# One megakernel of two attention, expert and feed-forward layers on one Trainium2 core: grouped keys, more PSUM banks for the experts, the convolution as matmuls

## The reference, cut to what matters

```python
x = x + attn0(cond(x, mask, cond_256, Wq, Wk, Wv, Wo, ...))     # cond: 16 heads of 8; attn0: 16 heads of 64, rotary, causal
x = x + moe0(rotate(x, ...))                                    # 8 experts, top 2, 128 -> 512 -> 128, relu
x = x + attn1(moe1(x, ...))                                     # moe1: 8 experts, top 2, 128 -> 256 -> 256 -> 128; attn1: 8 heads, decay
x = x + ffn(cond(x, ...))

def cond(...):                                  # in both places
    scores = einsum('bhsd,bhtd->bhst', q, k) * scale            # 16 heads of 8 features, 32 positions
    attn = softmax(where(mask, -inf, scores))
    out = einsum('bhst,bhtd->bhsd', attn, v) @ Wo.T
    return out / rms(out) * rms_scale * (1 + sc) + shift

def ffn(x, w1, conv_w, conv_b, w2):
    h = bit_linear(x, w1)            # row of x rounded to 127 steps of its largest value, weights to -1, 0, 1; 128 -> 512
    h = silu(depthwise_conv1d(h, conv_w, conv_b))               # 3 taps along the 32 positions
    return bit_linear(h, w2)                                    # 512 -> 128
```

## Time and profile before

| what | us |
|---|---|
| median of 3 runs (lowest, highest) | 674.3 (670.13, 675.94) |
| the profiled execution's own time | 680.54 |
| span of the profiled execution, first to last instruction | 678.7 |
| busy: PE, PEld, DVE, ACT, POOL | 468.1, 363.8, 350.4, 269.8, 212.3 |
| mean granted TensorE clock | 0.825 of 2.4 GHz |

### The profile page before, as it was taken

How to read it: one execution, slowest core, us unless ns; L and a number is a source line. 1 busy time by engine, 2 the same in 40 slices (tenths; PEclk the granted TensorE clock), 3 DMA queues, 4 the chain that set the end, 5 groups by cost and what they waited for, 6 DMA issues and landing times.

```text
span 678.7 us, 11047 instructions
## 1 busy us (share of the span) xinstructions
PE 468.1 (69%) x3753; PEld 363.8 (54%) x3753; DVE 350.4 (52%) x827; ACT 269.8 (40%) x729; POOL 212.3 (31%) x212
## 2 busy tenths in 40 slices
PE   2778697875888882767676775758888478574622
PEld 2556475663777771546555664636667256351311
DVE  2187877646353534520001005783754668988853
ACT  0324344422465641214443544213676355323322
POOL 1425435145142315460004004644122522434100
PEclk9999798985899995659988999776999768865555
DMA  9630000001153441025567663001555100000000
GB/s 320 181 105 2 0 2 1 1 1 41 53 156 91 138 125 47 24 87 170 167 182 194 194 176 92 12 27 29 157 160 153 35 10 1 4 1 0 5 4 8
DMA packets 79014, 53.58 MB, mean 79 GB/s; under 512 B 14608, under 2 KB 72912, under 8 KB 78704
## 3 DMA queue, kind: packets, MB, share of 16 engines
q1 hardware_dynamic: 76432, 48.37, 24.8%
q0 software_dynamic: 2048, 4.20, 2.1%
q10 hardware_dynamic: 480, 0.32, 0.2%
HBM read 44.34 MB, written 8.52 MB: 78 GB/s over the span
## 4 chain that ended last, share of the span: by engine, by line
PE 34%; DVE 23%; issue 10%; ACT 9%; POOL 4%; SPq 2%; another core or an unknown queue 2%; DMA 1%; POOLq 0%; DVEq 0%; ACTq 0%
PE PS L749 6%; PE PS L739 4%; DVE cond_ptbd L1164 4%; PE PS L1277 4%; PE PS L723 3%; PE PS L1245 2%; ACT hid L820 2%; DVE arena L1570 2%; PE PS L735 2%; PE PS L1523 2%; DVE arena L1736 1%; PE PS L1065 1%; PE PS L1268 1%; ACT arena L1693 1%
## 5 line engine op out<-in xcount | busy, mean ns | idle before, releaser
L1019 POOL TENSOR_TENSOR cond_kbd<-cond_qkv,const 128x2048 f32<-128x2048 f32 x16 | 59.6, 3724 | 19.4 <-ACT cond_qkv L1106 13.7
L749 PE MATMUL PS<-expert_w,hid 128*128 128x128 f32 x360 | 56.0, 294 | 13.1 <-ACT hid L820 10.5
L749 PEld LDWEIGHTS PS<-expert_w,hid 128*128 128x128 f32 x360 | 46.9, 199 | 22.3 <-issue 20.3
L820 ACT ACTIVATE hid<-PS,expert_b 128x128 f32<-128x128 f32 x120 | 37.5, 365 | 45.3 <-PE PS L739 28.2
L665 POOL DMA_INDIRECT picked<-slots_y,place_u x32 | 31.3, 977 | 74.7 <-DMA slots_y<-slot_y 65.9
L1164 DVE STREAM_TRANSPOSE cond_ptbd<-cond_sm 32x512 f32<-32x512 f32 x64 | 45.0, 703 | 2.4 <-PE PS L1077 1.2
L723 PE MATMUL PS<-slot_xT,expert_w 128*128 128x128 f32 x240 | 40.1, 292 | 7.5 <-issue 6.2
L812 ACT ACTIVATE hid<-PS,expert_b 128x128 f32<-128x128 f32 x120 | 37.6, 367 | 16.3 <-PE PS L723 14.8
L970 DVE SCALAR_TENSOR_TENSOR acc<-picked,weight,acc 128x128 f32<-128x128 f32 x8 | 2.8, 350 | 76.9 <-issue 70.3
L739 PE MATMUL PS<-hid,expert_w 128*128 128x128 f32 x240 | 36.1, 297 | 8.8 <-ACT hid L812 4.3
L1077 PE MATMUL PS<-cond_ptbd,cond_vbd 128*32 128x128 f32 x512 | 22.6, 332 | 24.0 <-DVE cond_ptbd L1164 24.0
(11 more groups left out here) (278 smaller groups left out, 1080.4 us busy)
## 6 DMA issues: line engine op xcount, KB each, us to landing
expert_w<-in_moe_w_dram SPq DMA_DIRECT2D x90, 256.0 KB
expert_w<-in_moe_w_dram SPq DMA_DIRECT2D x60, 128.0 KB
slot_x<-slots_x SPq DMA_DIRECT2D x60, 64.0 KB
slots_y<-slot_y SPq DMA_DIRECT2D x60, 64.0 KB
slots_x<-zeros SPq DMA_DIRECT2D x2, 960.0 KB, 6.4
rot_qk<-in_attn_qk_dram SPq DMA_DIRECT2D x1, 1024.0 KB, 8.2
arena<-in_attn_qk_dram SPq DMA_DIRECT2D x1, 1024.0 KB, 8.8
expert_b<-in_moe_b_dram SPq DMA_DIRECT2D x60, 2.0 KB
```

The costliest lines, as they stand in the source:

```text
L749: mm = nc.tensor.matmul(full(MO_[job], 2 * P, 3 * P), hid[:, i % 2, c, :], W[i % WB][:, lo + E * (c - first):lo + E * (c - first) + E], st ...
L820: ins = nc.scalar.activation(hid[:, i % 2, 2 + c, :], full(MB_[job_of(i)[0]], P * c, P * c + P), ACT.Relu, bias=WBIAS[i % WB][:, 2 + c:3 + c])
L1019: nc.gpsimd.tensor_tensor(ckbd[:], cqkv[s][:, P:2 * P].unsqueeze(1).to_broadcast([P, CH, P]), k["headmask"].unsqueeze(2).to_broadcast([P, ...
```

## The change

The names are those of the diff. What it does:

1. Keys: `spread_keys` writes the keys out 4 times, not 16 (128x512, two buffers `cond_kx`), each time with one head of every group of four. `scores` multiplies group by group: a 32-row part of the queries by the same rows of the keys, 16 matmuls of 32x32 by 128 columns. Ahead of each group but the first TensorE waits for its own previous group (`c_rows_step`). `spread_values` and the zeroed buffer are gone: `turn` is one block transpose into a plain `cond_pT`, `times_values` takes the values as they are, again four by four with such waits, and its output holds for each of four heads of a group a 128-column part, of which a masked output weight (`cond_wo`) picks the right rows: `project_o` has four matmuls in place of one. `spread_output` makes this weight on GpSimd, for both layers; its due times are 0 for layer 0 and 1.1 for layer 1, ahead of the first `c0_spread_keys` (6.1), and it waits for the load of that layer's weights (`cond_w1`: the last but the expert weights in SyncE's order).
2. Experts: the banks come from tables for each job and for even and odd slots. Jobs 0 and 3 keep banks 1 and 7. In the order transpose, `hidden_a`, `hidden_b`, output, even slots of job 1 use banks 2, 0, 7, 6 and odd ones 3, 1, 4, 5; in job 2 they are 2, 0 or 1, 7, 6. In jobs 1 and 2 the relus of half b run on VectorE (`relu_v`). Gates and routers get banks 2 or 7, and the order puts `m_transpose_u` and the `log_*` steps of tokens 0 to 511 before the end of job 2.
3. Feed-forward: the quantised row is turned by one f32 matmul with [shifted identity, identity, shifted identity] into three shifted transposes (`f_transpose_x`, 384 columns); `hidden` is one one-row matmul for the bias and three f32 matmuls of 512 columns, with weights that hold w1 times each tap (`taps_w`, made once: `f_spread_taps` on GpSimd, `f_taps_of_all` on TensorE, `f_scale_taps` on VectorE, 4 steps each, due at 67.8 to 100.8). Its output has tokens on partitions, so the four transposes back are gone. Silu is h(1 + tanh(h/2)), ScalarE's tanh and one VectorE instruction (`gate`). Banks: 6 for the turns and, in tiles 4 to 7, bank 1 for `hidden`; a tile no longer waits at its start for the sum of the tile before.
4. `level_weights` copies only the columns that a level can have (32, 31, 30, 28, 24 and 16 of 32).
5. TIMES is new throughout, so the order on every engine is. The zeroing of `cond_ptbd` and VectorE's wait for it are gone.

```diff
+        MT_, MA_ = ((1, 1), (2, 3), (2, 2), (1, 1)), ((1, 1), (0, 1), (0, 1), (1, 1))
+        MB_, MO_ = ((7, 7), (7, 4), (7, 7), (7, 7)), ((7, 7), (6, 5), (6, 6), (7, 7))
+        MM_ = (7, 7, 2, 7)
+        MX_, MU_ = (7, 7), (2, 7)
...
+            def relu_v(m):
+                i = RELU_V[m]
+                dve.wait_ge(m_b_ps, i + 1)
+                if i >= 2:
+                    dve.wait_ge(m_out_ps, i - 1)
+                for c in range(2):
+                    ins = nc.vector.tensor_scalar(hid[:, i % 2, 2 + c, :], full(bank_of(MB_, i), P * c, P * c + P), WBIAS[i % WB][:, 2 + c:3 + c], 0.0, ALU.add, ALU.max)
+                ins.then_inc(m_bv_ready, 1)
...
+            def spread_output(_):
+                if layer == 0:
+                    pool.wait_ge(loaded["cond_w0"], 16)
+                else:
+                    pool.wait_ge(loaded["cond_w1"], 16)
+                nc.gpsimd.tensor_tensor(cwo[layer][:], cond_w[layer][:, 3 * E:4 * E].unsqueeze(1).to_broadcast([P, HG, E]),
+                                        k["ofgroup"].unsqueeze(2).to_broadcast([P, HG, E]), ALU.mult).then_inc(c_wo_ready, 1)
...
-                if base + n:
-                    pool.wait_ge(c_scores_ps, base + n)
-                nc.gpsimd.tensor_tensor(ckbd[:], cqkv[s][:, P:2 * P].unsqueeze(1).to_broadcast([P, CH, P]),
-                                        k["headmask"].unsqueeze(2).to_broadcast([P, CH, P]), ALU.mult).then_inc(c_kbd_ready, 1)
+                if base + n >= CS:
+                    pool.wait_ge(c_scores_ps, base + n - CS + 1)
+                nc.gpsimd.tensor_tensor(ckx[s][:], cqkv[s][:, P:2 * P].unsqueeze(1).to_broadcast([P, HG, P]),
+                                        k["ofgroup"].unsqueeze(2).to_broadcast([P, HG, P]), ALU.mult).then_inc(c_kx_ready, 1)
...
             def scores(n):
+                for g in range(4):
+                    r = slice(S * g, S * g + S)
+                    if g:
+                        pe.wait_ge(c_rows_step, own_rows.next())
+                    for b in range(SEQ):
+                        mm = nc.tensor.matmul(full(bank, P * g, P * g + P)[S * b:S * b + S, :], cqkv[s][r, S * b:S * b + S], ckx[s][r, :, S * b:S * b + S], start=True, stop=True)
+                    mm.then_inc(c_rows_step if g < 3 else c_scores_ps, 1)
+            def times_values(n):
+                for b in range(SEQ):
+                    r = slice(S * b, S * b + S)
+                    if b:
+                        pe.wait_ge(c_rows_step, own_rows.next())
                     for g in range(4):
+                        mm = nc.tensor.matmul(full(bank, P * b, P * b + P)[S * g:S * g + S, :], cqkv[s][r, 2 * P + S * g:2 * P + S * g + S],
+                                              cpT[s][r, 4 * g:4 * g + 4, :], start=True, stop=True)
+                    mm.then_inc(c_rows_step if b < 3 else c_oT_ps, 1)
...
-                nc.tensor.matmul(full(COND_BANKS[layer][n], 2 * P, 3 * P), coT[s][:], w[:, 3 * E:4 * E], start=True, stop=True).then_inc(c_z_ps, 1)
+                for h in range(HG):
+                    mm = nc.tensor.matmul(full(COND_BANKS[layer][n], 2 * P, 3 * P), coT[s][:, h].rearrange("p b t -> p (b t)"), cwo[layer][:, h, :],
+                                          start=(h == 0), stop=(h == HG - 1))
...
-                for b in range(SEQ):
-                    last = nc.vector.transpose(cptbd[S * b:S * b + S, :, S * b:S * b + S], csm[s][S * b:S * b + S, :, :])
-                last.then_inc(c_probsT_ready, 1)
+                nc.vector.transpose(cpT[s][:], csm[s][:]).then_inc(c_probsT_ready, 1)
...
+        FX, FH = (6,) * TILES, (6,) * HT + (1,) * HT
+            def transpose_x(n):
+                pe.wait_ge(xd_ready, n + 1)
+                claim(pe, (FX[n],), (turned_ready, n + 1))
+                nc.tensor.matmul(full(FX[n], 0, 3 * P), xd, taps_id, start=True, stop=True).then_inc(turned_ps, 1)
             def hidden(n):
+                claim(pe, (FH[n],), (z_ready, n + 1))
+                nc.tensor.matmul(full(FH[n]), k["ones"][0:1, :], conv_b, start=True, stop=False)
+                for tap in range(3):
+                    mm = nc.tensor.matmul(full(FH[n]), xT3[:, tap, :], taps_w[:, tap, :], start=False, stop=(tap == 2))
+                mm.then_inc(inner_ps, 1)
+            def tanhs(n):
+                nc.scalar.activation(tz[n % 2], full(FH[n]), ACT.Tanh, scale=0.5).then_inc(tanh_ready, 1)
+            def gate(n):
+                nc.vector.scalar_tensor_tensor(out=tz[n % 2], in0=tz[n % 2], scalar=1.0, in1=full(FH[n]), op0=ALU.add, op1=ALU.mult).then_inc(z_ready, 1)
```

More of the change, by code:

```diff
@@ L74, in constants @@
     c["ident"] = np.eye(P)
+    c["tap_back"], c["tap_on"] = (same & (t[:, None] == t[None, :] + m) for m in (-1, 1))
     c["ones"] = np.ones((P, P))
@@ L738, in hidden_b @@
                             lo = FF1 + FF1 * c + P * f
-                            mm = nc.tensor.matmul(full(MB_[job], P * f, P * f + P), W[i % WB][:, lo:lo + P], hid[:, i % 2, c, :], start=(c == 0), stop=(c == 1))
+                            mm = nc.tensor.matmul(full(bank_of(MB_, i), P * f, P * f + P), W[i % WB][:, lo:lo + P], hid[:, i % 2, c, :], start=(c == 0), stop=(c == 1))
                 mm.then_inc(m_b_ps, 1)
@@ L957, in add_biases @@
                 rows = slice(HT * half, HT * half + HT)
-                bias = full(7).rearrange("p (n e) -> p n e", e=E)
+                bias = full(MM_[job]).rearrange("p (n e) -> p n e", e=E)
                 if layer == 0:
@@ L1060, in scores @@
             def scores(n):
-                s = n % CS
-                pe.wait_ge(c_kbd_ready, base + n + 1)
-                for b in range(SEQ):
-                    mm = nc.tensor.matmul(full(COND_BANKS[layer][n])[S * b:S * b + S, :], cqkv[s][:, S * b:S * b + S],
-                                          ckbd[:, :, S * b:S * b + S], start=True, stop=True)
-                mm.then_inc(c_scores_ps, 1)
-            def times_values(n):
-                s = n % CS
-                pe.wait_ge(c_probsT_ready, base + n + 1)
-                pe.wait_ge(c_vbd_ready, base + n + 1)
-                for m in range(4):
+                s, bank = n % CS, COND_BANKS[layer][n]
@@ L1706, in ffn_vector @@
+            return [("f_copy_xT", copy_xT), ("f_tanhs", tanhs), ("f_copy_yqT", copy_yqT)]
         def ffn_vector(dve, own):
[L1707 to L1725 removed]
```

576 lines of the change are left out of this document (290 added, 286 removed), and 87 rows, old and new, of the table TIMES.

## The result

The changed kernel takes 687.29 us (median of 4 runs, 682.28 to 691.90) where the kernel before, beside it on the same chip, takes 672.55 (670.13 to 675.94). The ratio is 1.0214, with a 95% interval of 1.0124 to 1.0304. The forecast was 624, with a range up to 652, so it was wrong in sign too. The change is slower clear of noise; whether it is slower by 2% isn't.

What follows compares the result with a forecast made beforehand. No engine was taken to bound the whole kernel; each stage had its own limit. Terms -9 - 2 - 8 - 6 + 3 - 8 - 21 = -51 took the span from 678.7 to 627.7, a median of 624 us, range 602 to 652.

Steps and rivals of the forecast that it cites:

- the gain on VectorE and the chain is 8 x 2.1 = 17: First stage, 23.3 to 156: eight small-attention tiles each save 2.1 us; less 5 and 3, the stage gets -9.
- 3 for the taps: First stage: preparing the taps adds 4.5 us on TensorE, half taken by idle time; 3 with the other engines' part.
- rival (d): TensorE becomes the bound, with 78 us more work: 728 at worst, median 684 with half in idle time; chance 0.04.
- Keys 1.17 and turn 0.71 for four of 0.703: Small attention: a tile's keys fall from 3.72 to 1.17 us on GpSimd, four transposes of 0.703 become one of 0.71.
- VectorE would stall less: Small attention: VectorE instructions wait for GpSimd's key writes; shorter writes of 1.17 us can cost a third.
- TensorE +2.3 a tile: Small attention: waits add 0.8 us in each of two steps, three more projection matmuls 0.7.
- The price of the wait: Small attention: each wait of TensorE for itself costs 0.26 us, read from one row; three in each of two steps.
- The start, +5: First stage: GpSimd's wait for layer 1's output weight delays the first scores to 37.4 from 32.29; cost taken as 5 us.
- Jobs 1 and 2, -8: Expert slots, 296 to 409: separate banks let TensorE near its busy time; a quarter of 31 us, range 0 to -15.
- The last stage, -21: 605 to the end: feed-forward tiles overlap, -10.6; earlier turns -4.2, stall 4.15, taps off VectorE 2.3; range -14 to -27.
- Silu's tables: ScalarE: five table loads of 1.28 us, 6.4 in all, may go; counted as no gain because they precede the data.
- a bound with TensorE as the limit: First stage, 23.3 to 156: its slow-side bound, 8 x 2.3 + 4.5 less most of TensorE's 26.8 idle, +4.

Runs made afterwards that it cites:

- e3: The changed kernel with the masked output weight of layer 1 made at due time 60 instead of ahead of the first keys: 684.04 us, ratio 1.0152.
- e9: The kernel before with the matmuls of scores, product with the values and output projection issued twice in each small-attention tile: 686.74 us, ratio 1.0238.
- e11: The kernel of e7 with one block transpose, the product with the values in four groups and four masked projection weights: 676.74 us, ratio 1.0082.
- e7: The kernel before in its own order, with the new banks, relus of half b on VectorE and shorter level weights: 672.60 us, ratio 0.9960.
- e12: The changed kernel with bf16 instead of f32 operands in the four 512-column matmuls of the convolution: 660.74 us, ratio 0.9839.
- e16: The changed kernel with hidden of tiles 4 to 7 in bank 3 and feed-forward of tiles 5 to 7 due like tile 4's: 706.28 us, ratio 1.0192.
- e10: The kernel of e7 with the grouped keys and the scores group by group, the rest of the small attention as before: 662.95 us, ratio 0.9883.

## Why the prediction was wrong

**The step that failed** is the one that lets TensorE's work lie beside other work: "the gain on VectorE and the chain is 8 x 2.1 = 17" in the first stage, and so in most stages after. TensorE was already at 105.9 of 132.7 us there, the fullest engine by 16 us, and the change gave it 19 more, of which I charged 3 for the taps and nothing for the rest, so long as the tile's path got shorter. The stage grew by 11, of which 4.3 are the wait at the start (e3) that I had charged with 5; where I had -14 for all else, +7 came. e9 shows the same without the change around it: its first scatter is 6.8 us later than before (162.9 for 156.1), and a us of TensorE issued costs 0.4 us over the kernel. I had this as rival (d) and gave it 0.04, since its "133 - 106 us idle" looked like room. In e9 and e11 the idle time took up only part of such work. The sum of (d) with half of the 78 in idle time, a span of 689 and a median of 684, came near the 689.8 and 687.29 measured, and that is in part luck: it had 37 us for the small attention, where 47.7 came, and it left out all savings but the tail's 21 and the jobs' 8, of which 6 came.

**Point by point.**
- Keys 1.17 and turn 0.71 for four of 0.703: right, 1.11 and 0.711. That VectorE would stall less: right. The subtraction took at most 0.98, where it had reached 2.82:

```profile
L1193 DVE TENSOR_TENSOR cond_sm<-cond_sm,cond_mx x16: 691/692/976, 41.2 to 644.4; 128x512 f32<-128x512 f32 x16
```

- TensorE +2.3 a tile: 3.0 on average, and 2.4 at full clock. The scores and the product cost 0.9 more each at either clock, for 0.8 forecast, and the projection 0.67 for 0.7 at full clock, so the sizing by pipelining held there; at half clock it is 1.28, and 13 of 16 ran so. What the term lacked is the clock. The copy of the product on ScalarE, 0.60 for 0.28, was not in the sum at all. The price of the wait was read wrongly, though the sum came out: 0.26 was a gap, while here a group of four small matmuls starts 0.51 after the one before it.
- The start, +5: right, scores at 36.8 for 37.4 forecast (33.7 in e3), and 4.3 us at the first scatter by e3.
- Jobs 1 and 2, -8: -3.5 in the changed kernel with the log steps among them; -4.8 in e7 without, from first scatter to first gather. Direction right by these two stretches, size half. That a quarter of the bound was to be had wasn't from a row.
- The last stage, -21: -2.5. The size of the convolution was nearly right (5.5 and 7.2 in the rows above, between my 4.5 and 8.2), its one-row bias matmul is as long as the others (888 and 890 ns), and the pitch of the tiles fell to 3.1 and 2.1 us from 13.9. What was wrong is what stands behind xn of tile 7: I placed tile 6's convolution ahead of it at 646.0 to 654.2, as if TensorE and the bank were free then. Three of them came after it. e12 gives most of the missing gain back by their length alone; e16 shows that the bank's wait is not it.
- Silu's tables, counted at nothing: the changed kernel loads a table 5 times, for 14 before, so 9 x 1.28 = 11.5 us of ScalarE went, and none of the 5 is at the tanh (L1738). This bears out what the Trainium skill ("ScalarE: Activation LUTs", "Table sets: the hidden batching unit") says, that tanh is in the set of exp. What the loads are worth in time wasn't tried; ScalarE was nowhere the limit.
- The range ended at 652 because it left out rival (d), the only one with all of TensorE's 78 us in it. The first stage had a bound with TensorE as the limit, but set at +4, where +11 came.

**What stays open:** how much of the cost is a full queue and how much a longer path; why the clock was at half for more of the small attention than before, and what that cost; whether the two halves of the small attention cost more together than apart, and what the best order for the changed parts would give; only two orders were run.

## What to carry to other kernels

Before moving work from other engines to one, read that engine's busy share stage by stage. On a TensorE queue that was busy for 69% of the span and for 80% of the first stage, a us issued in the small attention cost 0.4 us (e9), and one taken out of the convolution gave 0.9 (e12), while 41 us saved on GpSimd for 12 of TensorE gave some 5 (e10). Ask of each exchange how many us it takes off and puts on: the grouped keys (41 of GpSimd for 12) came out ahead or even, the turn with its projection (30 of VectorE and 19 of GpSimd for 32) lost. And price a part in the order that the kernel already had, since here undoing a part in the order written for it made parts look good that cost time.

## What the runs showed of the hardware

- TensorE's granted clock was higher where more work was given, in two places. In the last stage, where it was 0.50 with TensorE busy for 32.3 of 73.7 us, the changed kernel has 0.62 with 55.7 of 71.2. In e9, whose only change is more TensorE work, the mean over the span is 0.860 for 0.825 (0.855 to 0.862 in its runs, 0.815 to 0.842 in those of before beside them), so part of the added work probably paid for itself. It is no rule of busy time alone: in the sixth slice of the pages above TensorE is 9 tenths busy in both kernels, with the clock at 0.9 before and at 0.5 in the changed one. What lowered it there wasn't tried.
- A set of four 32x32 by 128-column f32 matmuls on the same rows of the array, followed by a wait for itself, takes 0.51 us at 2.4 GHz (the rows at 609.52 and 610.03) and 0.74 at 1.2 (four are 2.86 long, the last 0.65), far from twice: an estimate from these two is that 0.28 of it doesn't change with the clock.
- A record of a 512-column f32 matmul took 592 ns at least and 1222 at most, and each matmul has two; a bf16 one has one record, of 379 to 634. From the start of a tile's bias matmul to the end of its third tap the changed kernel takes 3.9 us at full clock and 7.5 at half, e12 1.14 and 1.98. So the operand type was worth a factor of three to four in TensorE time.
